# Leaving the self-loops of a graph out of the gathers, in a message-passing kernel on one core

## What is computed

```python
all_msgs = jnp.einsum('nh,thd->ntd', h, message_W) + message_b
msg = all_msgs[src, edge_type]
messages = jax.ops.segment_sum(msg, dst, num_segments=num_nodes)
gi = messages @ gru_w_ih.T + gru_b_ih
gh = h @ gru_w_hh.T + gru_b_hh
# r, z: sigmoid of gi + gh; n = tanh(i_n + r * h_n)
# h' = (1 - z) * n + z * h;  out = layernorm(x + h')
```

## Time and profile before

| | |
|---|---|
| Device time, median of 3 runs | 2104.45 us (2103.55 to 2104.69) |
| The profiled execution | 2104.37 us, of it 2102.4 us span from the first to the last instruction |
| Mean granted clock of TensorE | 0.71 of full speed |
| PE busy | 1588.7 us (76%), 7483 instructions |
| PE weight loads | 1244.0 us (59%) |
| VectorE busy | 862.0 us (41%): 8.8 us a round |
| ScalarE busy | 558.3 us (27%) |
| POOL busy | 1572.9 us (75%), nearly all indirect DMAs |
| DMA engines, mean busy share | 0.23, 60 GB/s |

### The profile page before, as it was taken

The page is one execution under the profiler, slowest core; times in us unless marked ns, Lnnn a source line. Parts: engine busy times, 40 slices in busy tenths (PEclk is TensorE's granted clock), DMA queues, the critical chain, the costliest instruction groups (busy, mean ns, idle before and its releaser), DMA issues.

```text
span 2102.4 us, 32384 instructions
## 1 busy us (share of the span) xinstructions
PE 1588.7 (76%) x7483; PEld 1244.0 (59%) x7580; DVE 862.0 (41%) x3288; ACT 558.3 (27%) x1580; POOL 1572.9 (75%) x1672
## 2 busy tenths in 40 slices
PE   3777787777787877777777777787777777777776
PEld 3656565656565656656565656565656566555655
DVE  5343434434343434343434343434434343434344
ACT  3322222222222222222222222222222222222222
POOL 7777777777777777777777777777777777777774
PEclk9877667666767676767676767767777666776767
DMA  6222222222222222222222222222222222222221
GB/s 115 57 58 60 57 60 57 60 57 60 57 61 58 60 57 60 57 60 57 59 59 57 60 58 61 58 60 57 60 57 60 57 60 57 60 57 60 58 59 42
DMA packets 91709, 125.42 MB, mean 60 GB/s; under 512 B 33338, under 2 KB 65120, under 8 KB 91696
## 3 DMA queue, kind: packets, MB, share of 16 engines
q0 software_dynamic: 53152, 108.96, 20.5%
q1 hardware_dynamic: 35182, 16.29, 3.0%
q10 hardware_dynamic: 3362, 0.01, 0.2%
HBM read 118.74 MB, written 6.40 MB: 60 GB/s over the span
## 4 chain that ended last, share of the span: by engine, by line
POOL 41%; issue 26%; DMA 14%; PE 12%; ACT 5%; ACTq 1%; POOLq 0%; DVE 0%; DVEq 0%
POOL rows L424 41%; DMA rows<-in_x_dram,idx 13%; PE agg L1008 6%; ACT sums L530 3%; PE msg L1021 3%; ACT idx L497 1%; PE gates L1042 1%; PE gates L1038 1%; PE msg L1018 1%; DMA round_dst<-in_dst_dram 0%; ACT agg L522 0%; PE gates L1039 0%; ACTq L486 0%; PE cnt L996 0%; POOLq L443 0%
## 5 line engine op out<-in xcount | busy, mean ns | idle before, releaser
L424 POOL DMA_INDIRECT rows<-in_x_dram,idx x1644 | 1554.5, 946 | 502.5 <-issue 466.5
L1008 PE MATMUL agg<-onehot,rows 128*128 128x128 f32 x3288 | 820.5, 377 | 315.5 <-DMA rows<-in_x_dram,idx 301.0
L1008 PEld LDWEIGHTS agg<-onehot,rows 128*128 128x128 f32 x3288 | 582.3, 243 | 499.8 <-issue 470.9
L530 ACT ACTIVATE sums<-agg 128x512 f32<-128x512 f32 x293 | 173.1, 591 | 1058.0 <-PE agg L1008 1058.0
L818 DVE TENSOR_TENSOR t_rh<-rz,gates 128x128 f32<-128x128 f32 x96 | 27.6, 288 | 688.1 <-ACT rz L566 688.1
L1021 PE MATMUL msg<-sums,w_type 128*128 128x192 f32 x1568 | 296.4, 346 | 0.0
L1021 PEld LDWEIGHTS msg<-sums,w_type 128*128 128x128 f32 x1568 | 291.7, 211 | 0.0
L996 PE MATMUL cnt<-node_mask,type_mask 128*128 128x16 bf16 x1661 | 179.2, 180 | 136.4 <-issue 130.6
L766 DVE TENSOR_TENSOR onehot<-type_f,codes 128x768 f32<-128x768 f32 (+1 forms) x293 | 264.5, 903 | 0.0
L996 PEld LDWEIGHTS cnt<-node_mask,type_mask 128*128 128x128 bf16 x1661 | 136.0, 98 | 210.7 <-issue 180.0
L522 ACT ACTIVATE agg<-zeros_f 128x512 f32<-128x512 f32 x294 | 176.6, 601 | 9.2
(11 more groups left out here) (144 smaller groups left out, 890.7 us busy)
## 6 DMA issues: line engine op xcount, KB each, us to landing
rows<-in_x_dram,idx POOLq DMA_INDIRECT x1644, 2.5
x_next<-in_x_dram SPq DMA_DIRECT2D x97, 64.0 KB
out_dram<-out_tile SPq DMA_DIRECT2D x97, 64.0 KB
dst_rows<-in_dst_dram SPq DMA_DIRECT2D x1, 704.0 KB
src_rows<-in_src_dram SPq DMA_DIRECT2D x1, 704.0 KB
type_rows<-in_edge_type_dram SPq DMA_DIRECT2D x1, 704.0 KB
w_type<-in_L_gnn_message_W_dram SPq DMA_DIRECT2D x1, 512.0 KB
rows_second<-in_x_dram,idx_second POOLq DMA_INDIRECT x17, 2.5
```

What stands on the lines that cost most here:

```text
L424: nc.gpsimd.indirect_dma_start(out=rows[:, k, :], out_offset=None, in_=x[:, :], in_offset=bass.IndirectOffsetOnAxis(ap=idx[:, k:k + 1], ax ...
L530: read = nc.scalar.activation(sums[:, :, c, :], agg[c][:, :].rearrange("p (n t) -> p t n", t=TYPES), ACT.Copy)
L1008: last = nc.tensor.matmul(agg[c][:, ds(offs[k] * TYPES, CODES)], (rows_second if second else rows)[:, START[c] + k, :], onehot[c][:, k, :] ...
```

## The change

Every edge that is a self-loop and the last of its run is left out of the gathers; its message is made from x itself, which the kernel has anyway for the node update.

- The first 170 tiles (10 rounds of 17, `EARLY`) are left as they were, loops included. The other 190740 edges are laid in 118 rows of 1620 edges, one row on each partition, and **packed on the chip**: `rise` to `worst` find the loops and check the form (6 steps), `shift` to `word` put source, type, kind of the next edge and distance into one 32-bit word for each edge, and 7 stages of `moves` and `moved` (a mask, then a `copy_predicated` by 1, 2, 4 ... 64 places) close the gaps. 12 tiles of 128 are left of each row, 1416 in all. Each step is six instructions of 270 columns on VectorE (`pack`). `prepare(r)` puts them into rounds 1 to 7, behind the messages' adds.
- In rounds 8 and 9 PE turns the four fields of the words in 12 pieces (`turn_field`), and ScalarE copies them (`copy_field`). From round 10 on a round has 16 tiles (6, 5, 5); there are 88 such rounds and a last one with 6 tiles: 170 + 1408 + 6 = 1584 tiles.
- An edge in front of a left-out loop carries the loop's type as its second kind (`kinds_T`), and the count product gives 8 more rows: which type each node's loop has. VectorE adds these to `loops_T` (`add_loops`); ScalarE copies 128 nodes of it (`copy_loops`), PE spreads each type's row over the partitions (`spread_loops`, 4 products after group 0 and 4 after group 1), and VectorE multiplies them with the turned x (`loop_x`). The result stands as 128 more columns beside the sums, so that `apply_weights` has 320 columns; `make_messages` adds the part of the loops to the messages.
- x is turned in the free quarter of the counts' bank (`xt = cnt[:, 3*P:4*P]`), one round behind; `gates` is alone in its bank; `x_tile` is loaded from memory a second time instead of copied.
- All counts of a round (`count_tiles`) stand in front of the sums, and the node update (`finish_pre`, `finish_out`) stands first on VectorE, in front of the messages' adds.
- The last round is another: 6 tiles, the loops' products by themselves, and node tiles 95, 96 and 97 finished one after another (before, the last two side by side).

The core of it:

```diff
-            for c in range(3):
-                gather_group(1, c)
-            gather_second_round()
+            pool.wait_ge(src_ready, 1)
+            for c, n, start in groups(0):
+                gather_early(0, c, n, start)
...
+                pool.wait_ge(src_ready, 3)
+                for r in range(2, EARLY):
+                    for c, n, start in groups(r):
+                        gather_early(r, c, n, start)
+                gather_packed(1)
+                with pool.Fori(2, ROUNDS - EARLY) as due:
+                    gather_packed(due)
+                gather_packed(ROUNDS - EARLY, 1)
```

```diff
+            def pack(name, make, width=6 * PIECE, size=PIECE, one_by_one=False):
+                base = AT[name] - 6
+                for i in range(6):
+                    a, b = i * size, width if i == 5 else (i + 1) * size
+                    wait_used(dve, packing, base + i if one_by_one and i else base - 6 + min(i + 2, 6) if base else 0)
+                    make(i, a, b).then_inc(packing, 1)
...
+                pack(f"moves{stage}", lambda i, a, b: nc.vector.tensor_scalar(
+                    moves_row[:, a:b], word_row[:, a:b], 1 << (SHIFT + stage), None, ALU.bitwise_and))
+                pack(f"moved{stage}", lambda i, a, b: nc.vector.copy_predicated(
+                    word_row[:, a:b], moves_row[:, a + d:b + d], word_row[:, a + d:b + d]),
+                    ROW_EDGES - d, one_by_one=True)
```

VectorE's round:

```diff
             def round_(r):
-                masks(r, 1)
-                if since(r, LAG + 1):
-                    finish_pre(r - LAG - 1)
-                masks(r, 2)
-                add_messages(r - 1)
-                if since(r, LAG + 1):
-                    finish_out(r - LAG - 1)
-                masks(r + 1, 0)
+                make_onehot(r, 1)
+                make_onehot(r, 2)
+                if since(r, LAG + 1):
+                    finish_pre(r - LAG - 1)
+                    finish_out(r - LAG - 1)
+                if since(r, 1):
+                    add_messages(r - 1, msg)
...
+                if since(r, EARLY - 1):
+                    add_loops(r)
+                if since(r, EARLY + 1):
+                    make_messages(r - LAG, r)
+                if since(r, EARLY):
+                    loop_x(r - 1, 0)
+                    loop_x(r - 1, 1)
...
+                if not since(r, EARLY):
+                    prepare(r)
+                small_masks(r + 1)
+                make_onehot(r + 1, 0)
```

PE's product with the weights:

```diff
             def apply_weights(r):
...
+                if loops_too:
+                    wait_loops(r)
+                cols = TURNED if loops_too else APPLIED
                 for t in range(TYPES):
-                    last = nc.tensor.matmul(out_cols, w_type[:, t, :], sums[:, t, 0:groups, :].rearrange("p c n -> p (c n)"),
-                                            start=False, stop=t == TYPES - 1)
+                    nc.tensor.matmul(msg[:, 0:cols], w_type[:, t, :], sums[:, t, 0:cols], start=t == 0, stop=False,
+                                     skip_group_check=True)
```

and between the groups:

```diff
+            def spread_loops(r, h):
+                pe.wait_ge(loops_ready, r - (EARLY - 1))
+                if h == 1:
+                    pe.wait_ge(loop_x_ready[0], r - (EARLY - 1))
...
+                for t in range(4):
+                    last = nc.tensor.matmul(turn[:, t * P:(t + 1) * P], spread[:, 4 * h + t, :], loops[:, :], start=True, stop=True)
+                last.then_inc(spread_done[h], 1)
```

More of the change, by code:

```diff
@@ new lines, in _ @@
+            sp.dma_start(dst_row[LOOSE:whole - 1, ROW_EDGES:WIDE], rows_of(dst, LOOSE + 1, whole)[:, 0:OVER]).then_inc(dst_in, 16)
+            follow = min(OVER, ROW_REST)
+            sp.dma_start(dst_row[whole - 1:whole, ROW_EDGES:ROW_EDGES + follow], line(dst, rest, rest + follow)).then_inc(dst_in, 16)
+            sp.dma_start(dst_row[whole:ROWS, 0:ROW_REST], line(dst, rest, EDGES)).then_inc(dst_in, 16)
+            with nc.allow_non_contiguous_dma(reason="the edge in front of each row, once"):
+                sp.dma_start(dst_before[0:ROWS, :],
+                             dst[EARLY_EDGES - 1:EDGES:ROW_EDGES].rearrange("(r c) -> r c", c=1)).then_inc(dst_in, 16)
@@ L377, in _ @@
                 load_bias()
-                with sp.Fori(0, PAIR[0] - 1) as j:
-                    load_x(j + 1)
-                    store_out(j)
-                store_out(PAIR[0] - 1)
-                store_out(PAIR[0], s=of(PAIR[0]))
-                store_out(PAIR[1], NODE_LAST, of(PAIR[1]))
+                load_x(1)
+                sp.wait_ge(packing, AT["next"])
+                with nc.allow_non_contiguous_dma(reason="the kind of the edge that follows the early ones"):
+                    sp.dma_start(kinds_T[P - 1:P, EARLY_TILES - 1, 1:2], moves_f[0:1, 0:1]).then_inc(carried, 16)
@@ new lines, in _ @@
+            copy(src_T[:, EARLY_ROUND:P], turn[:, EARLY_ROUND:P]).then_inc(src_ready, 1)
+            with nc.allow_non_contiguous_dma(reason="the first dst of every early edge tile, once"):
+                act.dma_start(first_early[0:1, :],
+                              dst[0:EARLY_EDGES:P].rearrange("(p e) -> p e", p=1)).then_inc(first_in, 16)
+            extra = EARLY_TILES - P
+            act.wait_ge(early_src_in, 16)
+            copy(src_f[0:extra, 1, :], src_e[0:extra, 1, :]).then_inc(src_f_ready, 1)
@@ L565, in finish_rz @@
                 act.wait_ge(gates_ready, j + 1)
[L566 removed]
+                if not s:
+                    wait_used(act, zd_ready, j)
+                nc.scalar.activation(rz[s][:, :], gates[:, 0:2 * HID], ACT.Sigmoid).then_inc(rz_ready, 1)
             def finish_n(j):
@@ L1010, in sum_tiles, with wait_loops @@
+                    last = nc.tensor.matmul(agg[c][:, ds(offs[c][k] * TYPES, CODES)],
+                                            (rows_second if second else rows)[:, start + k, :],
                                             onehot[c][:, k, :], start=False, stop=True, skip_group_check=True)
                 last.then_inc(tiles_done[c], 1)
-            def apply_weights(r, groups=3):
-                pe.wait_ge(sums_copied[groups - 1], r + 1)
+            def wait_loops(r):
+                for h in range(2):
+                    pe.wait_ge(loop_x_ready[h], r - (EARLY - 1))
+                if since(r, EARLY + 1):
+                    pe.wait_ge(messages_ready, r - 1)
```

1310 lines of the change are left out of this document (813 added, 497 removed).

## The result

The changed kernel takes **2046.3 us** (median of 4 runs, 2044.9 to 2048.3) against 2104.4 us for the kernel before on the same chip: ratio 0.9725, 95% interval [0.9708, 0.9742]. The prediction was 2029, with 2015 to 2082 as the range. The profiled execution took 2046.9 us for a span of 2045.2. So the way and the main term are right, and 17 us more are spent than I had laid out.

A forecast was written before the change was run, and what follows sets the result against it. POOL's gather issue, 1.249 us each, was taken as the bound. 1584 gathers plus start, packing 5, seam 2, small adds 0.5 and tail 35 gave a span of 2026.7, forecast 2029 us; 8-in-10 range 2015 to 2082, its own 2015 to 2048.

The forecast's parts named there:

- Fewer gathers: POOL issues 1584 gathers for 1661 at 1.249 us each: 96.2 us less, a packed round 20.0 us.
- TensorE in a packed round: Group 0's indices ready 15.1 us after S, the round's first gather, wanted at S+20.0; margin shrinks from 9.5 to 4.9 us.
- the handshake's wait: After group 0 PE waits 1.6 us for the loops' counts from ScalarE, covered by the wait for rows.
- A grant near 1.00 while the 320 columns run: Sign to look for: TensorE's granted clock near 1.00 during the products with the weights.
- The start: The checks' flag comes at 32 to 36 us; nothing lost, cover of 6 to 10 us.
- The 2.5 us that the sum kept for the start: Loss at the start of the kernel before, carried unchanged into the forecast sum.
- The packing: VectorE's 174 pieces hold up gathers that start inside two-input ones, 0.13 us on average: 5 us.
- rival B's second form: POOL gets no turn within a whole stretch of packing pieces, 56 us of pieces: 2080 us; chance 0.05.
- my zero for them: One-input packing pieces taken to cost POOL's gathers nothing, with up to 16 us as the other end.
- The seam: Rounds 8 and 9, turning the packed fields and clearing the loops' table: 2 us once, between nothing and 8.
- The tail: The end comes 35 us after the last gather, 22.0 before: 13 us lost, between 8 and 20.

The follow-up runs named there:

- e9_half_products: Changed kernel with seven of sixteen onehot products left out in each packed round, all gathers still issued: 2046.7 us, ratio 0.9726 to the kernel before.
- e1_kinds: Kernel before with stretches of 24 added VectorE pieces, eight kinds, each twice, in rounds 4 to 19: 2744.4 us against 2751.7 on a slower chip.
- e12_twelve: Changed kernel with 12 gathers in each full packed round in place of 16: 2371.2 us on a slower chip (kernel before 2747.8).

## Why the prediction was right, and where it was off

- **Fewer gathers, 96.2 us; a round 20.0.** Right: 1.250 us a gather over 1397 gathers, starts 20.0 apart from round 11 on.
- **TensorE in a packed round.** Indices said for S+15.1, wanted at S+20. The rows of the last full round, S = 1988.4:

```profile
1994.60 6.18 PE L1390 MATMUL msg<-sums_room,w_type 128*128 128x320 f32 x16 [1.07 <-issue]
...
2001.46 1.58 PE L1369 MATMUL agg<-onehot,rows 128*128 128x128 f32 x12
...
2003.08 0.60 ACT L636 ACTIVATE sums_room<-agg 128x512 f32<-128x512 f32 x1 [0.63 <-PE agg L1369]
...
2004.25 0.19 ACT L636 ACTIVATE idx<-src_T 128x6 int32 x1
...
2004.94 0.39 PE L1411 MATMUL turn<-loops,spread 16*128 16x128 bf16 x4 [1.90 <-ACT loops L636]
```

  S+16.0, 0.9 later. The 16 passes took 6.18 instead of 5.0 us, at a grant of 0.72 (1994.60 to 2000.40), and started only after a wait of 1.07; the handshake's wait (1.9 for 1.6) and the counts (0.55 for 0.8) were near. In the next round the passes took 4.54 and the grant stood at 1.00. "A grant near 1.00 while the 320 columns run" was thus half right: it came in the middle of them in one round and ahead of them in another. The margin is 4.0 where 4.9 was said, and nothing of it was used up: after its first gather POOL waited over 0.3 us for indices at the seam alone, and e9_half_products with less work on TensorE took the same time.
- **The start.** Flag said for 32 to 36, ready at 33.5 (fits at 33.48). ScalarE had read group 0's sums by 44.2 and POOL asked at 55.8, late by its own stall. The 2.5 us that the sum kept for the start were gathers held up beside the old checks (2.57 us at 8.09); in the changed kernel these losses are part of the packing's.
- **The packing: the step that failed.** Said 5 us, measured 18.6 (9.1 + 5.2 + 3.4 + 0.9). For the gathers that enter between pieces the term was right: 0.08 to 0.26 us each, 5.4 us in all. The other 13.2 us are two gathers that got no turn within a stretch. This is rival B's second form, to which I gave 0.05, in two stretches, not in all. I had one row against it, the gather of 56.69: it got in between two instructions, but both were on one partition, so it was a case of another sort. One row of the nearest kind carried the whole exclusion.

  The Trainium skill (SBUF — State Buffer, Who interferes with whom) says that the shared port pair is an exclusive lock and that whoever issues first holds it for the whole instruction, the other fully blocked. The traces agree for a single instruction (2.57 us beside the subtraction of the earlier trace rows), and show more than that: over 24 instructions in a row a waiting gather got no turn (8.65 us), while beside the same pieces elsewhere it got one after each (1.10 us). It also says that tensor-scalar forms in a 2-port mode block GpSimd for the whole instruction. In the profile after gathers beside the one-input pieces of round 7 took 1.02 to 1.03 us, 0.1 more than alone, so my zero for them was nearly right there; the 5.53 us of e1_kinds beside pieces of 0.21 us is again more than one instruction's time.
- **The seam: mis-sized.** Said 2 us with 8 as the far end, measured 13.0, of it 11.6 in waits for indices. Three rows had no counterpart before and I took them by the width alone:

```profile
202.70 4.23 ACT L636 ACTIVATE work<-work 118x1536 f32<-118x1536 int32 x3
...
222.79 1.33 ACT L636 ACTIVATE kinds_T<-turn 128x472 f32<-128x472 f32 x1
224.89 1.34 ACT L636 ACTIVATE kinds_T<-turn 128x472 f32<-128x472 f32 x1 [0.78 <-PE turn L1441]
...
243.38 5.34 DVE L1203 MEMSET work<- 16x6336 uint32 x1 [5.31 <-issue]
```

  The casts (1.4 each for 1.7 said) and the clearing (5.34 for 5.4) were right. But a copy of 472 columns that scatters its result takes 0.97 to 1.34 us where 512 columns in a row take 0.60, and with PE's turn (0.6 to 1.0) and the two handshakes a pair is 1.75 to 2.5 us, not 1.25: some 25 us for the twelve and not 15. The clearing then waits 5.31 us for the last of them, the offsets for the clearing, and PE's round 10 for the offsets. A chain of 15 us became one of 25, and its cover was that of 15.
- **The tail.** Said 35 us behind the last gather, measured 30.5 (2014.69 to 2045.2; 22.0 before). The products for 64 columns ended at S+22.2, not S+29: loops' handshakes and gates overlapped more than I let them. In their place VectorE was late; its update of the tile before, held up 1.83 us for x_tile, pushed the last add to 2033.91, and PE waited 3.94 for the messages:

```profile
2034.51 1.65 PE L1425 MATMUL gates<-w_ih_T,messages 128*128 128x384 f32 x2 [3.94 <-DVE messages L1033]
```


The sum, then: + 13.6 (packing), + 11.0 (seam), + 1.3 - 0.5 - 2.5 (rate over the packed rounds, small adds, start), - 4.5 (tail): 18.4 of the 18.5 us between the forecast span of 2026.7 and 2045.2.

That 2046.3 lies just inside the forecast's own range (2015 to 2048) is in part luck. Its upper end was made of other ends (one-input pieces up to 16 us, seam up to 8, tail up to 20) than what came, and without the 4.5 us by which the tail was shorter than said the time would lie above it.

## What to carry to other kernels

Where an engine's instructions are the bound by a constant rate, fewer of them is worth exactly that, and the risk sits in the few places where the others hold it up once. VectorE work laid beside a gather-bound POOL wants a gap now and then: a long stretch of pieces back to back, above all behind an instruction on few partitions, can hold one gather for its whole length. Price a copy by how it scatters, not by its columns, and multiply a hand-to-hand chain by its full turn. A margin of 4 us in 20 was safe on one chip and gone on others, where a round waits 8 us for indices.

## What the runs showed of the hardware

- A gather's issue, 0.94 us alone, takes 0.94 to 1.22 beside VectorE pieces that let it in (e1_kinds) and up to 9.62 when they don't (e12_twelve, gather of 15.70); a gap of 0.16 us was enough to let it in.
- A TensorE with 15% fewer matmuls (691 for 811 in 200 us, e9_half_products) was busy equally long, the grant falling from 0.88 to 0.74.
- Chips of the same kind ran the kernel before in 2104 us and, three of them, in 2748 to 2797, with the same 0.94 us per gather; in the traces of the slower ones engines stand for 1.3 to 9 us in front of instructions with nothing to wait for. A ratio measured on one didn't carry over to another (0.9725 and 0.9973).
- On the slower chips VectorE was through with the checks at 32 to 33 us where a gather had stood still before, and at 49 to 54 where gathers went on, in five runs each.
